# A graph kernel with 125 chunks of edges: a new opening, and node sums that are turned among the last main matmuls

## What is computed

```python
diff = (u[dst] - u[src]) * inv_dx[:, None]
d1 = jax.ops.segment_sum(diff, dst, num_segments=N) - jax.ops.segment_sum(diff, src, num_segments=N)
S = jax.ops.segment_sum(slope_edge, dst, num_segments=N)
dt_c = jnp.clip(dt, DT_MIN, DT_MAX)
u_next = u - dt_c * (u * d1 + g * S)
...
sums = jax.ops.segment_sum(edge_attr, dst, num_segments=nb_node)
return sums / denom[:, None]
...
x = _layernorm(x + _L0_gnn_ref(x, edge_index, edge_attr_2, L0_gnn_dt, L0_gnn_g), axis=-1)
x = _layernorm(x + _L1_gnn_ref(x, edge_index, edge_attr_16), axis=-1)
```

## Time and profile before

| | us |
|---|---|
| median of 3 runs | 5270.9 |
| the runs | 5274.25, 5255.2, 5270.9 |
| the profiled execution | 5260.41 |
| its span | 5258.6 |
| busy in it: TensorE, VectorE, GpSimd, ScalarE | 4753.0, 3926.8, 3418.5, 1444.4 |
| mean granted clock of TensorE, as a share of full speed | 0.947 |
| first main matmul starts | 121.42 |
| last main matmul ends | 5199.58 |

### The profile page before, as it was taken

How to read it: one execution, slowest core, us unless ns; L and a number is a source line. 1 busy time by engine, 2 the same in 40 slices (tenths; PEclk the granted TensorE clock), 3 DMA queues, 4 the chain that set the end, 5 groups by cost and what they waited for, 6 DMA issues and landing times. The chain is left out here.

```text
span 5258.6 us, 90500 instructions
## 1 busy us (share of the span) xinstructions
PE 4753.0 (90%) x31379; PEld 2860.2 (54%) x31380; DVE 3926.8 (75%) x8584; ACT 1444.4 (27%) x1014; POOL 3418.5 (65%) x3133
## 2 busy tenths in 40 slices
PE   1999999999999999999999999999999999999996
PEld 0555555555555555555555555555555555555554
DVE  3777777777777777777777777777777777777776
ACT  3322232222322232223222232223222232222320
POOL 5666666666666666666666666666666666666660
PEclk9999999999999999999999999999999999999998
DMA  2111111111111111111111111111111111111110
GB/s 72 30 30 38 30 30 30 30 38 30 30 30 38 30 30 30 38 30 30 30 30 38 30 30 30 38 30 30 30 30 38 30 30 30 38 30 30 30 28 7
DMA packets 210186, 167.92 MB, mean 32 GB/s; under 512 B 124538, under 2 KB 193662, under 8 KB 209912
## 3 DMA queue, kind: packets, MB, share of 16 engines
q1 hardware_dynamic: 109734, 139.79, 8.1%
q0 software_dynamic: 100000, 25.80, 4.7%
q10 hardware_dynamic: 428, 2.01, 0.1%
HBM read 164.55 MB, written 2.81 MB: 32 GB/s over the span
## 5 line engine op out<-in xcount | busy, mean ns | idle before, releaser
L588 PE MATMUL ps_src<-hi_hot,spread 128*128 128x391 bf16 x25000 | 4684.2, 338 | 240.2 <-issue 204.4
L380 POOL DMA_INDIRECT x_src<-in_x_dram,src_i x3125 | 3413.5, 1092 | 1696.5 <-issue 853.8
L588 PEld LDWEIGHTS ps_src<-hi_hot,spread 128*128 128x128 f16 x25000 | 2201.2, 99 | 1613.2 <-issue 342.0
L876 DVE TENSOR_SCALAR hi_hot<-col_h,hi_f,scale 128x1564 bf16<-128x1564 f16 x3125 | 2256.3, 726 | 966.5 <-PE ps_src L588 911.9
L537 PE MATMUL ps_w<-dst_of_node,parts 128*102 128x112 bf16 x3125 | 690.2, 222 | 134.1 <-issue 100.7
L808 DVE TENSOR_TENSOR spread<-lo_rows,halves 128x640 f16<-128x640 f16 x1250 | 623.1, 499 | 80.5 <-issue 80.5
L537 PEld LDWEIGHTS ps_w<-dst_of_node,parts 128*102 128x102 bf16 x3125 | 412.8, 133 | 432.6 <-issue 256.9
L526 PE MATMUL ps_x<-xwin,node_of_dst 112*128 112x48 bf16 x3125 | 596.2, 193 | 49.8 <-issue 38.6
L443 ACT CAST parts<-pay 128x425 bf16<-128x425 f32 x125 | 72.6, 581 | 1747.3 <-DVE pay L768 1747.3
L526 PEld LDWEIGHTS ps_x<-xwin,node_of_dst 112*128 112x128 bf16 x3125 | 316.4, 102 | 268.3 <-issue 106.1
L466 ACT ACTIVATE node_of_dst<-rel_all,row_neg 128x3200 bf16<-128x3200 f16 x125 | 369.9, 2959 | 10.7 <-DMA rel_all<-rel_d 10.7
(11 more groups left out here) (112 smaller groups left out, 1044.3 us busy)
## 6 DMA issues: line engine op xcount, KB each, us to landing
rel_all<-rel_d SPq DMA_DIRECT2D x125, 800.0 KB
x_src<-in_x_dram,src_i POOLq DMA_INDIRECT x3125
a<-in_edge_attr_dram SPq DMA_DIRECT2D x125, 200.0 KB
a<-in_edge_attr_dram SPq DMA_DIRECT2D x125, 25.0 KB
src_i<-in_src_dram SPq DMA_DIRECT2D x125, 12.5 KB
dst_i<-in_dst_dram SPq DMA_DIRECT2D x125, 12.5 KB
xwin<-xparts_d SPq DMA_DIRECT2D x125, 10.5 KB
dst_sum<-in_dst_dram SPq DMA_DIRECT2D x1, 1562.5 KB
```

The lines of the kernel that those rows point to most:

```text
L380: nc.gpsimd.indirect_dma_start(x_src[:, b, j * F:(j + 1) * F], None, x[:, :], bass.IndirectOffsetOnAxis(ap=src_i[:, b, j:j + 1], axis=0)). ...
L588: last = nc.tensor.matmul(ps_src[:, q, 0:HB], spread[:, b, j, k, :, :].rearrange("p l f -> p (l f)"), hi_hot[:, slot(b, j), q * HB:(q + 1) ...
L876: v.tensor_scalar(hi_hot[:, slot(b, j), :], col_h[:, :], hi_f[:, b, j:j + 1], scale[:, b, j:j + 1], ALU.is_equal, ALU.mult).then_inc(hi_ho ...
```

## The change

**In the opening,** the transfers of dst, x, `rel_d` and `xparts_d` that had 125 partitions are issued as two each, of 112 (`SIXTEENS`) and 13. VectorE takes the least dst ahead of the third part of x, not after it. ScalarE clears the large piece of `dst_sum` after the x parts, stores the zero rows of `xparts_d` ahead of the others, makes chunk 0's `lo_rows` first in `finish(0)`, and does the attributes of chunk 1 ahead of `node_hot(2)`. Stages -2 and -1 of VectorE have lists of their own, `FIRST_PIECES` and `SECOND_PIECES`.

**In every stage,** the four operations on `src_i` (L769, L770, L776, L779 of before) are one piece "lo" after `pay`; the last three stood among those of `scale`.

**At the end,** the 13 groups of transposes stand in the last stage behind tiles 2 to 14 (`turn_sums`), VectorE's sums behind its `hi_hot` of tiles 5 to 17 (`part_sums`). The part of the update that needs no src sums (`known`) is computed ahead of `src_done`; the copies out of `ps_src` are shared by ScalarE and VectorE; the operations after them run over halves of 6 and 7 of the 13 blocks, with the squares on ScalarE; the result goes out in one more piece.

`spread` and `lo_rows` are one buffer now (`spread_lo`), so that `sum_f` has its place behind the half that the last stage reads; `attr` and `known` lie in `dst_of_node` and `node_of_dst`. `op` issues an operation and waits for it; `stats(q, i)` and `blocks(t, i)` are half i of a tensor. The lists and SyncE's part:

```diff
-                  6: ["pay"], 7: ["scale"], 8: ["scaled"], 9: ["left"], 10: ["parts"],
+                  6: ["pay", "lo"], 7: ["scale"], 8: ["scaled"], 9: ["left"], 10: ["parts"],
...
+        FIRST_PIECES = {0: ["dst_rel"] + ["dst_hot"] * 5 + ["slope", "attr_left", "attr_parts"]}
+        SECOND_PIECES = {0: ["dst_rel"] + ["dst_hot"] * 5 + ["x_of_dst", "lo", "diff", "pay", "scale", "scaled", "left", "parts", "slope"] +
+                            ["spread"] * 6 + ["window", "attr_left"] + ["spread"] * 4 + ["attr_parts"]}
...
-            sp.dma_start(dst_all, dst.rearrange("(c e) -> c e", e=CH)).then_inc(dst_all_loaded, 16)
+            dst_rows = dst.rearrange("(c e) -> c e", e=CH)
+            sp.dma_start(dst_all[0:SIXTEENS, :], dst_rows[0:SIXTEENS, :]).then_inc(dst_all_loaded, 16)
+            sp.dma_start(dst_all[SIXTEENS:C, :], dst_rows[SIXTEENS:C, :]).then_inc(dst_all_loaded, 16)
...
-            sp.dma_start(rel_d, rel_split).then_inc(rel_stored, 16)
-            sp.wait_ge(rel_stored, 16)
+            sp.dma_start(rel_d[0:SIXTEENS, :], rel_split[0:SIXTEENS, :]).then_inc(rel_stored, 16)
+            sp.dma_start(rel_d[SIXTEENS:C, :], rel_split[SIXTEENS:C, :]).then_inc(rel_stored, 16)
+            sp.wait_ge(rel_stored, 32)
...
-            sp.wait_ge(xparts_stored, 48)
+            sp.wait_ge(xparts_stored, 64)
...
+                sp.wait_ge(pay_ready if isinstance(n, int) and n == 0 else lo_ready, n + 1)
```

ScalarE's part:

```diff
-            act.dma_start(x_rows, x.rearrange("(p n) f -> p (n f)", p=XR)).then_inc(x_loaded, 16)
-            act.wait_ge(zeros_ready, 1)
-            nc.scalar.copy(dst_sum[:, CLEAR[1]:PADN], zeros[:, 0:1].to_broadcast([P, PADN - CLEAR[1]])).then_inc(sums_clear, 1)
...
+            act.dma_start(x_rows[0:SIXTEENS, :], x_all[0:SIXTEENS, :]).then_inc(x_loaded, 16)
+            act.dma_start(x_rows[SIXTEENS:XR, :], x_all[SIXTEENS:XR, :]).then_inc(x_loaded, 16)
+            act.wait_ge(x_loaded, 32)
...
-            act.wait_ge(xparts_ready, 1)
-            act.dma_start(xparts_d[0:NODES, :].rearrange("(p n) q -> p (n q)", p=XR),
-                          x_split.rearrange("p n k f -> p (n k f)")).then_inc(xparts_stored, 16)
+            act.wait_ge(zeros_ready, 1)
             act.dma_start(xparts_d[NODES:NODES + P, :], zeros[:, 0:SPL * F]).then_inc(xparts_stored, 16)
             act.dma_start(xparts_d[NODES + P:PADN, :], zeros[0:PADN - NODES - P, 0:SPL * F]).then_inc(xparts_stored, 16)
+            act.wait_ge(xparts_ready, 1)
+            act.dma_start(xparts_rows[0:SIXTEENS, :], split_rows[0:SIXTEENS, :]).then_inc(xparts_stored, 16)
+            act.dma_start(xparts_rows[SIXTEENS:XR, :], split_rows[SIXTEENS:XR, :]).then_inc(xparts_stored, 16)
...
             nc.scalar.copy(dst_sum[:, 0:CLEAR[0]], zeros[:, 0:1].to_broadcast([P, CLEAR[0]])).then_inc(sums_clear, 1)
+            nc.scalar.copy(dst_sum[:, CLEAR[1]:PADN], zeros[:, 0:1].to_broadcast([P, PADN - CLEAR[1]])).then_inc(sums_clear, 1)
             act.wait_ge(dst_max_ready, 1)
             nc.scalar.copy(dst_sum[:, CLEAR[0]:CLEAR[1]], zeros[:, 0:1].to_broadcast([P, CH])).then_inc(sums_clear, 1)
...
+                if isinstance(n, int) and n == 0:
+                    act.wait_ge(lo_ready, 1)
+                    nc.scalar.copy(lo_rows[:, :, :, :], bc(lo_hot[:, :, :], 3, F)).then_inc(lo_rows_ready, 1)
...
                 nc.scalar.copy(parts[:, :, 1, 0:F + 1], left[:, :, 0:F + 1]).then_inc(part1_ready, 1)
-                act.wait_ge(lo_ready, n + 1)
-                nc.scalar.copy(lo_rows[:, :, :, :], bc(lo_hot[:, :, :], 3, F)).then_inc(lo_rows_ready, 1)
+                if not (isinstance(n, int) and n == 0):
+                    act.wait_ge(lo_ready, n + 1)
+                    nc.scalar.copy(lo_rows[:, :, :, :], bc(lo_hot[:, :, :], 3, F)).then_inc(lo_rows_ready, 1)
...
             finish(0)
+            begin(1, 0, 1)
             node_hot(2, 0)
-            begin(1, 0, 1)
```

TensorE's part:

```diff
+            def turn_sums(h):
+                n = min(P, HCOL - h * P)
+                if h == 0:
+                    pe.wait_ge(win_added, C)
+                if h >= 2:
+                    pe.wait_ge(fin_free, h - 1)
+                for l in range(LO):
+                    last = nc.tensor.transpose(fin_bank(h, l // HALF)[0:n, (l % HALF) * SPL * V:(l % HALF + 1) * SPL * V],
+                                               dst_sum[0:SPL * V, h * P * LO + l:h * P * LO + l + (n - 1) * LO + 1:LO],
+                                               ident[0:SPL * V, 0:SPL * V])
+                last.then_inc(fin_dst, 1)
...
+                    if not finish and 0 <= j - TURN_AT < HT:
+                        turn_sums(j - TURN_AT)
...
-                if h >= 2:
-                    pe.wait_ge(fin_free, h - 1)
-                for l in range(LO):
-                    last = nc.tensor.transpose(fin_bank(h, l // HALF)[0:n, (l % HALF) * SPL * V:(l % HALF + 1) * SPL * V],
-                                               dst_sum[0:SPL * V, h * P * LO + l:h * P * LO + l + (n - 1) * LO + 1:LO],
-                                               ident[0:SPL * V, 0:SPL * V])
-                last.then_inc(fin_dst, 1)
...
+                q = (h * P + n - 1) // HB
+                pe.wait_ge(src_in[0], q // 2 + 1)
+                if q:
+                    pe.wait_ge(src_in[1], (q + 1) // 2)
+                nc.tensor.transpose(turned_src[0:n, h if h < H2 else h + 8 - H2, :], src_t[:, h * P:h * P + n], ident[:, :]).then_inc(fin_ps, 1)
```

VectorE's part:

```diff
             v.tensor_tensor(x_rest, xr, x_split[:, :, 0, :], ALU.subtract).then_inc(xrest_ready, 1)
+            dve.wait_ge(dst_all_loaded, 32)
+            step(v.tensor_reduce(lim[0:C, 0:1], dst_all, AX, ALU.min))
             dve.wait_ge(xrest_ready, 1)
             dve.wait_ge(xpart1_ready, 1)
             v.tensor_tensor(x_split[:, :, 2, :], x_rest, x_split[:, :, 1, :], ALU.subtract).then_inc(xparts_ready, 1)
-            dve.wait_ge(dst_all_loaded, 16)
-            step(v.tensor_reduce(lim[0:C, 0:1], dst_all, AX, ALU.min))
             settle()
...
+                if piece == "lo":
+                    if isinstance(n, int) and n == 0:
+                        dve.wait_ge(src_loaded[0], 16)
+                    step(v.tensor_single_scalar(lo_i[:, :], src_i[:, b, :], LO - 1, ALU.bitwise_and))
+                    step(v.tensor_single_scalar(hi_i[:, :], src_i[:, b, :], LO.bit_length() - 1, ALU.logical_shift_right))
+                    settle_here()
+                    step(v.tensor_copy(hi_f[:, b, :], hi_i[:, :]))
+                    v.tensor_tensor(lo_hot[:, :, :], bc(lo_i[:, :], 2, LO), bc(col_i[:, 0:LO], 1, J), ALU.is_equal).then_inc(lo_ready, 1)
...
                     settle_here()
                     v.tensor_tensor(pay[:, :, 0:F], x_dst[:, :, :], bc(w[:, :], 2, F), ALU.mult).then_inc(pay_ready, 1)
-                    step(v.tensor_single_scalar(lo_i[:, :], src_i[:, b, :], LO - 1, ALU.bitwise_and))
-                    step(v.tensor_single_scalar(hi_i[:, :], src_i[:, b, :], LO.bit_length() - 1, ALU.logical_shift_right))
...
+            stage(-2, 0, 0, 0, False, False, True, FIRST_PIECES)
...
+            stage(-1, 1, 0, 0, False, True, True, SECOND_PIECES)
...
+            for j in range(J):
+                one_hot(C - 1, 0, j)
+                if j == 0:
+                    dve.wait_ge(hi_hot_free, (C - 1) * J + RING)
+                    fstep(v.memset(sum_f[:, HT - 1, :, :], 0.0))
+                if j == PART_AT:
+                    fsettle()
+                if 0 <= j - PART_AT < HT:
+                    part_sums(j - PART_AT)
...
             op(v.tensor_scalar(mean, sums[:, :, F], gdt[:, 1:2], None, ALU.mult))
-            dve.wait_ge(fin_ps, 1)
-            op(v.tensor_tensor(t3, sums[:, :, 0:F], s3, ALU.subtract))
...
-            op(v.tensor_tensor(t3, t3, bc(mean, 2, F), ALU.add))
-            op(v.scalar_tensor_tensor(t3, t3, gdt[:, 3:4], x3, ALU.mult, ALU.add))
-            op(v.tensor_tensor(u3, x3, t3, ALU.add))
-            def layer_norm():
-                op(v.tensor_reduce(mean, u3, AX, ALU.add))
-                op(v.tensor_scalar(mean, mean, 1.0 / F, None, ALU.mult))
...
+            op(v.tensor_tensor(k3, sums[:, :, 0:F], x3, ALU.mult))
+            op(v.tensor_tensor(k3, k3, bc(mean, 2, F), ALU.add))
+            op(v.scalar_tensor_tensor(k3, k3, gdt[:, 3:4], x3, ALU.mult, ALU.add))
+            op(v.tensor_tensor(k3, x3, k3, ALU.add))
+            dve.wait_ge(src_done, 1)
+            dve.wait_ge(hi_hot_free, C * J + RING)
+            for q in (1, 3):
+                v.tensor_copy(src_t[:, q * HB:(q + 1) * HB], ps_src[:, q, 0:HB]).then_inc(src_in[1], 1)
...
+            for i in range(2):
+                dve.wait_ge(fin_ps, H2 if i == 0 else HT)
+                got = turned_src[:, 0:H2, :] if i == 0 else turned_src[:, 8:8 + HT - H2, :]
+                op(v.scalar_tensor_tensor(blocks(tmp_all, i), nodes(got), gdt[:, 2:3], blocks(x_fin, i), ALU.mult, ALU.mult))
```

(13 more changed lines are left out.)

120 lines of the change are left out of this document (61 added, 59 removed).

## The result

After took 5249.07 us (median of 20 runs, 5235.01 to 5267.17), before 5261.57 (20 runs beside them, 5249.97 to 5274.73). The ratio is 0.9976 with a 95% interval of 0.9967 to 0.9985. So the change gained 12.5 us, 0.24%, where 29.4 were forecast. The time lies in the forecast range, but under half of the gain came, and it is less than the 0.5% that the prediction takes for no change.

What follows compares the result with a forecast made beforehand. TensorE's main matmuls were taken to bound the steady stages, so time could go only in the opening (18.4 us) and the tail (11.0). 5265.2 - 29.4 gave 5236 us; the range to hold 8 in 10 was 5197 to 5258.

Steps and rivals of the forecast that it cites:

- Transfers ahead of the row matmuls: Opening: transfers spread over more engines start the row matmuls at 35.5 instead of 51.24, 15.7 us earlier.
- If 23.0 us after the last instruction is the law: Opening: both x_dst_ready signs reach VectorE 23.0 us after its last instruction; main matmuls start at 103.0, gaining 18.4 us.
- tied to something that does not move: Rival, opening: VectorE's idle holes follow something like GpSimd's gathers; 0 to 2.6 us gained in front, total 5253, chance 0.21.
- Both holes close: Rival, opening: both VectorE idle holes vanish; main start as good as at 65, gain 55 there, total 5200, chance 0.18.
- From a release to the next `hi_hot`: Opening: VectorE's work from the first sign's release to the first `hi_hot`'s end takes 14.8 us, instead of 19.7.
- Stage 0 at its old length: First main stage: its length was taken as unchanged, without a term of its own.
- Every stage: cost 0: Steady stages: moving "lo" delays `parts` by about 0.35 us, covered by 2.2 us of slack, so cost 0.
- VectorE's chain outruns its slack: Rival, steady stages: `parts` 2.7 us later makes TensorE wait 0.5 us in each of 123 stages; 5297, chance 0.04.
- The end: Last stage and tail: 48.0 us, including 11.4 for transposes, against 59.0; gain 11.0, between 6 and 14.
- the lower clock: Last stage: transposes might halve TensorE's clock, costing 29 us more, 5265; its chance lies within the slower rival's 0.04.
- VectorE's 3.0 for the slope's factor: Last stage: this VectorE operation keeps its 3.0 us beside GpSimd's multiply; 0.3 would be the other end.
- The sum: Whole kernel: 18.4 us from the opening and 11.0 from the end make 29.4 us gained.

Runs made afterwards that it cites:

- gather_late: After, with GpSimd's gather of chunk 1 held until x_dst_ready was raised once; 5159.87 us in a single run, where before took 5055.98.
- gated: After, with the four `src_i` operations at their old places and the gathers of chunks 1 and 2 each waiting for an x_dst_ready; 5028.45 us, ratio 0.9944.
- split: paced, with chunk 1's gather pausing after 10 DMAs until the second x_dst_ready and chunk 2's paced by stage 0's tiles; 5106.85 us, ratio 0.9684.
- no_gather: After without its 3125 indirect DMAs, so the result lacks x of the src nodes; 4515.66 us, ratio 0.8925.
- push: After, with eight matmuls of zeros behind each of the opening's two bursts of row matmuls; 5268.02 us, ratio 0.9991.
- after_again: After unchanged, run once more on another chip; 5267.26 us, ratio to before 0.9984.
- no_lo_again: After, with the four `src_i` operations at their old places; 5245.23 us, ratio to before 0.9942.
- paced: gated, with each indirect DMA of the loop waiting for its own tile (GROUP 1 for 5) and AHEAD 20 for 10; 5118.08 us, ratio 0.9698.

## Why the prediction was wrong, step by step

**Transfers ahead of the row matmuls: right in kind, too large.** Least dst 13.58, not 10.5: it waited 2.86 us for its load. The store of `rel_d` took 4.4 us from its issue to the load behind it, not 3.6, against 8.2 before, with 63.3% of 16 engines in 25:29 where the old one had 27.6% in 33:40. Timelines of VectorE and SyncE:

```profile
13.58 3.49 DVE L743 TENSOR_REDUCE lim<-dst_sum 125x1 f32<-125x3200 int32 x1 [2.86 <-DMA dst_sum<-in_dst_dram]
...
24.68 0.35 SPq L333 DMA_DIRECT2D rel_d<-spread_lo  x1
...
29.07 0.36 SPq L314 DMA_DIRECT2D rel_all<-rel_d  x1
```

The row matmuls came at 39.6, not 35.5: 11.6 us earlier, not 15.7, inside the bounds. The split itself works. It agrees with what the Trainium skill says in "DMA: Bandwidth & Descriptors", section "Why a DMA increments its semaphore by 16 and not by 1": a transfer gets the largest number of engines up to 16 that divides its slowest dimension. The advice in the Trainium skill's section "Rules for kernel authors" on the same page, against two transfers to disjoint halves, is about halves that both use all 16 engines. Taken for 125 rows it would have left nothing of the store's 3.8 us. What part of the 11.6 us is the split's, and what part the moved clear's and the new order's, no run parts.

**"If 23.0 us after the last instruction is the law": the step that failed.** It isn't. The holes are tied to GpSimd's gathers: they vanish where none is under way (the first sign of gather_late and gated, both of split and no_gather), they stay with more work behind the burst (push), and their length varies between executions of one kernel. Two equal numbers in one profile, 22.99 and 23.02, were taken for a rule, and the forecast main start of 103.0 met 102.67 only by the sum of two wrong terms, the transfers 4.1 us too early and the holes 4.5 too long. That was luck. The rival "tied to something that does not move" named the gathers and was the right mechanism, but its price was too simple: a sign also got through in the middle of a gather (at 57.5 in after_again, at 100.4 in after), and then the later work went slower. Its total, 5253, came nearest to 5249, but by luck as well: it had 0 to 2.6 us in front and nothing in the loop, where the front gave 12.0 and the loop took most of that. *Both holes close* forecast a start at 65 and 55 us gained; split and no_gather do start at 63.3 and 61.6, but with the gathers still to be done the 55 would not have come, as split's first two stages show.

**From a release to the next `hi_hot`: right.** Forecast 14.8, measured 74.29 to 89.19, 14.9.

**Stage 0 at its old length: wrong.** It was never a term. 7.5 us of the 18.7 were given back there, because the main matmuls now ran into chunk 2's gather. That is the same cause a second time: whoever moves TensorE's work ahead of a gather's end moves it into the gather. With 0.8 won back in stage 1, the front gave 12.0 and not 18.4, and 3.8 in after_again.

**"Every stage: cost 0": the second step that failed, by 11 to 22 us on these chips.** This is the larger miss, and with it falls the prediction's first paragraph, by which time could go only in the opening and in the tail. The medians' 12.5 us leave 11.1 for the loop beside 12.0 in front and 11.6 at the end; the table gives 15.3, and after_again and no_lo_again 22.0. The slack of 2.2 us was there, and VectorE never became the bound: no wait for `hi_hot` stands among TensorE's of after in 160:4900. So the rival "VectorE's chain outruns its slack" named the right place but not what happened. What grew is TensorE's idle behind its own issue, 330.0 to 358.3 us, and it moved from the window sums to the main matmuls. The runs show that the place of the four operations costs this time, that this idle time stands at GpSimd's long rows of indirect DMAs, and that it goes away with the gathers (no_gather). How the order on VectorE brings it about, they don't show.

**The end: right.** Forecast 11.0, measured 11.6. The last stage took 44.4 us, and in before 33.3 (5166.3 to 5199.6), so 11.1 more (forecast 11.4), at clock 1.00, so the lower clock that the Trainium skill's page "TensorE: Matmul & The Clock Gate", section "Part 4: PE-mode transpose", would allow did not come. `known` was 4.0 us late, not 4.3 (ten tiles took 13.5 us, not 13.8). The tail behind the last matmul was 35.2, not 36.6: the output took 3.5, not 4.8. By these two terms the end would have given 12.7 (59.0 - 35.2 - 11.1); 1.1 went before the last stage, at whose start TensorE waited 0.98 us for VectorE's `hi_hot`, a wait that stood in no term. VectorE's 3.0 for the slope's factor stayed (3.03).

**The sum.** 29.4, less 6.4 in front, plus 0.6 at the end, less 15.3 in the loop, is 8.3; the medians gave 12.5, which takes a loop of 11.1.

**Open.** What in the chip holds TensorE's signs and paces its instructions while GpSimd issues indirect DMAs; why a sign sometimes gets through in the middle; why moving "lo" adds idle time, and why some eight times as much on gather_late's chip as on the others; whether pacing gains on a chip where before takes 5056 to 5061; and how much of paced's gain comes from its single steps and how much from its issuing 10 tiles later (AHEAD 20), since both were changed at once.

## What to carry to other kernels

An idle hole whose releaser the profile can't name, or an engine that waits in its own issue, is best read beside GpSimd's timeline: if a long row of indirect DMAs stands next to it, try pauses in that row, where another engine needs a sign. Work that is brought forward must be priced in its new surroundings, and not at the length that it had at its old place. And a piece of work that moves within a steady stage is no zero term: a small change of order, times 123, was as large here as the whole gain of the opening, and ten times as large in the one comparison on another chip. A gain of a quarter of a per cent should be measured on more than one chip.

## What the runs showed of the hardware

- While GpSimd issued indirect DMAs 1.25 us apart, VectorE sat idle up to 40.9 us for a sign of TensorE (gather_late; the last row matmul had ended at 60.1, the read came at 111.7). With none under way GpSimd went on 0.8 us after the last row matmul (gated, 40.5 and 41.4), and VectorE read with 0.59 us of idle.
- In the hole itself the DMA engines had little to do: in 44:76 of after the gathers took 7.4% of 16 engines and moved 0.18 MB.
- TensorE's small matmuls came 0.70 us apart in gated, and 2 to 3.5 us apart in after_again, in the midst of a gather; without the gathers no such step is seen. In the loop TensorE's idle behind its own issue stood at rows of 10 to 20 indirect DMAs (before 52.3 of 54.7 us, after 59.7 of 59.7, in 1000:1800).
- The 3125 indirect DMAs cost this kernel 545 us of 5061 (no_gather), though GpSimd was busy only 65% of before's span and TensorE 90%. Letting them go one at a time, 20 tiles behind and not 10, with the gates in the opening, won 127 us of 5245 on one chip (paced against no_lo_again).
- Before took 5262 to 5274 us on some chips and 5056 to 5061 on others, at mean clocks near 0.947 and 0.976.
